# Batch 0's first product by halves of the depth, over eight PSUM banks, from a second layout of W

## The reference

```python
# x: (8, 256, 1024) f32; weight: (8, 1024, 1024); ids: 8 adapter numbers, one for each batch
y      = einsum('bsi,boi->bso', x, weight[ids])          # first product, W of the batch's adapter
base   = einsum('bth,oh->bto', y, W_up)                  # second product, the same W_up for all
logits = y @ gate_w.T + expert_bias                      # 4 experts
z      = einsum('nh,erh->ner', y, lora_A)                # rank 8 for each expert
delta  = einsum('ner,ehr->neh', z, lora_B)[argmax(logits)]
out    = x + base + delta
```

## Time and profile before

| what | us |
|---|---|
| median of 3 runs (367.38 to 367.71) | 367.55 |
| profiled execution, its own time | 367.27 |
| its span | 365.5 |
| PE busy | 360.0 (99%) |
| DVE, ACT busy | 279.6 (77%), 159.6 (44%) |

### The profile page before, as it was taken

The page is one execution under the profiler, slowest core; times in us unless marked ns, Lnnn a source line. Parts: engine busy times, 40 slices in busy tenths (PEclk is TensorE's granted clock), DMA queues, the critical chain, the costliest instruction groups (busy, mean ns, idle before and its releaser), DMA issues.

```text
span 365.5 us, 5961 instructions
## 1 busy us (share of the span) xinstructions
PE 360.0 (99%) x2180; PEld 322.5 (88%) x2180; DVE 279.6 (77%) x554; ACT 159.6 (44%) x318; POOL 1.3 (0%) x11
## 2 busy tenths in 40 slices
PE   7999999999999999999999999999999999999996
PEld 5888988899888998889988898889988899888995
DVE  4777889999987886579856788477984788755773
ACT  5677445963345521565024651255413652144300
POOL 0000000000000000000000000000000000000000
PEclk9999999999999999999999999999999999999999
DMA  7999987871049802676037750486305871160003
GB/s 242 392 401 292 404 355 289 307 264 65 1 174 343 269 21 104 207 275 223 0 130 249 256 174 2 172 295 201 138 2 203 313 231 61 57 231 1 2 0 115
DMA packets 20252, 68.16 MB, mean 187 GB/s; under 512 B 2304, under 2 KB 2688, under 8 KB 20224
## 3 DMA queue, kind: packets, MB, share of 16 engines
q1 hardware_dynamic: 19936, 66.74, 51.0%
q10 hardware_dynamic: 288, 1.05, 0.9%
HBM read 59.39 MB, written 8.39 MB: 185 GB/s over the span
## 4 chain that ended last, share of the span: by engine, by line
PE 97%; SPq 1%; DMA 1%; DVE 0%; ACT 0%; issue 0%
PE ps_y L806 33%; PE ps_y L809 16%; PE ps_u L817 13%; PE ps_v L817 7%; PE ps_p L817 6%; PE ps_u L823 3%; PE ps_u L825 3%; PE ps_u L827 3%; PE ps_v L823 2%; PE ps_v L827 2%; PE ps_v L825 2%; PE ps_p L823 1%; PE ps_p L825 1%; PE ps_p L827 1%; DMA w_raw<-w_dram 1%; SPq L240 1%
## 5 line engine op out<-in xcount | busy, mean ns | idle before, releaser
L806 PE MATMUL ps_y<-x_hilo,w_hi 128*128 128x512 f32 x512 | 160.9, 396 | 0.5 <-DVE w_lo L497 0.5
L809 PEld LDWEIGHTS ps_y<-x_hilo,w_lo 128*128 128x128 f32 x512 | 96.2, 188 | 22.7
L809 PE MATMUL ps_y<-x_hilo,w_lo 128*128 128x256 f32 x512 | 100.6, 278 | 0.0
L504 DVE TENSOR_TENSOR w_lo<-w_raw,w_hi 128x512 fp32r<-128x512 f32 x126 | 81.2, 689 | 11.5 <-ACT w_hi L372 10.8
L806 PEld LDWEIGHTS ps_y<-x_hilo,w_hi 128*128 128x128 f32 x512 | 78.4, 189 | 1.4 <-DVE w_lo L497 0.9
L372 ACT CAST w_hi<-w_raw 128x512 fp32r<-128x512 f32 x126 | 71.8, 624 | 3.2 <-DMA w_raw<-w_dram 3.2
L387 ACT COPY small<-ps_y 128x256 f32<-128x256 f32 x64 | 23.9, 373 | 98.3 <-PE ps_y L809 98.3
L556 DVE TENSOR_TENSOR y_raw<-ps_y,small 128x256 f32<-128x256 f32 x64 | 27.1, 424 | 43.3 <-ACT small L387 43.3
L817 PE MATMUL ps_u<-wide_hi,y_parts 128*128 128x256 f32 (+1 forms) x256 | 46.2, 288 | 0.0
L817 PEld LDWEIGHTS ps_u<-wide_hi,y_parts 128*128 128x128 f32 x256 | 38.5, 188 | 0.7
L390 ACT CAST y_parts<-y_raw 128x512 fp32r<-128x512 f32 x53 | 30.6, 619 | 12.1 <-DVE y_raw L562 12.1
(11 more groups left out here) (94 smaller groups left out, 380.7 us busy)
## 6 DMA issues: line engine op xcount, KB each, us to landing
w_raw<-w_dram SPq DMA_DIRECT2D x64, 512.0 KB, 4.8
rows<-x_dram SPq DMA_DIRECT2D x16, 512.0 KB, 6.2
out_dram<-rows SPq DMA_DIRECT2D x15, 512.0 KB, 2.7
x_raw<-xT_dram SPq DMA_DIRECT2D x14, 512.0 KB, 5.0
wide_raw<-w_up_dram SPq DMA_DIRECT2D x4, 512.0 KB, 12.1
thin_raw<-w_up_dram SPq DMA_DIRECT2D x4, 512.0 KB, 13.0
wide_stage<-w_up_dram SPq DMA_DIRECT2D x4, 512.0 KB, 12.8
thin_stage<-w_up_dram SPq DMA_DIRECT2D x4, 512.0 KB, 8.2
```

The lines of the kernel that those rows point to most:

```text
L504: dve.tensor_tensor(w_lo[:, n % RAWS, part], w_raw[:, n % RAWS, part], w_hi[:, n % RING, part].bitcast(F32), ALU.subtract).then_inc(w_read ...
L806: pe.matmul(ps_y[c % 2][:, :], w_hi[:, n % RING, i * P:(i + 1) * P], x_hilo[:, :, i, :], start=(i == 0), stop=False)
L809: last = pe.matmul(ps_y[c % 2][:, S:2 * S], w_lo[:, n % RAWS, i * P:(i + 1) * P], x_hilo[:, 0, i, :], start=False, stop=(i == KC - 1))
```

## The change

- W for batch 0 comes from a new input, `w_halves`. Row n of an adapter (0 to 7) still has 128 partitions of 4 KB, but holds half of the depth (four steps of k) of two neighbouring blocks: rows 0 to 3 are k = 0 to 3 of blocks 0-1, 2-3, 4-5, 6-7, and rows 4 to 7 are k = 4 to 7 of the same. Row 0 comes in two transfers of 256 KB, one for each of its blocks, in pieces of 2 KB. All later batches use `w` as before.
- `open_product()` takes the place of `first_product(0)` on PE: the half h of the depth is outside, the block c inside, each block with a PSUM bank of its own: the six of `ps_u`, `ps_v`, `ps_p` and the two `ps_y`. Block 0's hi matmuls wait for the hi part alone. `half_done` counts pairs of blocks done in the first half, `block_done` whole blocks in the second.
- The waits for a free slot of `w_raw` or `w_hi` go by `wait_for_use`, which counts `half_done` for rows 0 to 3 and `block_done` by two for rows 4 to 7.
- ACT and DVE split row 0 as 256, 256 and 512 columns, then rows 1 and 2, then x 3, then rows 3, 4, 5, unit 0, row 6, unit 1, ahead of the product's loop. Row 7 is split at c = 0, unit 2 at c = 2, the gate's parts at c = 3.
- `plain(0)` also waits for six blocks read out (`y_full_ready` 6), since they lie in its banks. `y_small(0, c)` waits for block c-2's addition.
- `gl` is issued ahead of unit 3. `WARM` is 11, not 18.

```diff
+        ps_open = [ps[:, i, :] for ps in (ps_u, ps_v, ps_p) for i in range(2)] + [ps[:, :] for ps in ps_y]
+        def wait_for_use(engine, n):
+            if n < OC // 2:
+                engine.wait_ge(half_done, n + 1)
+            elif n < OC:
+                engine.wait_ge(block_done, 2 * (n - OC // 2) + 2)
+            else:
+                engine.wait_ge(block_done, n + 1)
-            i = load_blocks(0, 4, i)
+            for n in range(4):
+                load_pair(n, i)
             for n in range(4, OC):
                 load_unit(n - 4)
-                i = load_blocks(n, n + 1, i)
-            sp.dma_start(gl_raw[:, 0:2 * Q, :], gl[:, :, :]).then_inc(gl_in, 16)
+                load_pair(n, i)
+                if n == 6:
+                    sp.dma_start(gl_raw[:, 0:2 * Q, :], gl[:, :, :]).then_inc(gl_in, 16)
-            for q in range(QUARTERS // 2):
-                first_w_hi(q)
+            first_w_hi()
+            for n in (1, 2):
+                w_hi_part(n)
             x_hi(0, XQ - 1)
-            for q in range(QUARTERS // 2, QUARTERS):
-                first_w_hi(q)
-            for n in range(1, AHEAD):
+            for n in (3, 4, 5):
                 w_hi_part(n)
+            unit_hi(0)
+            w_hi_part(6)
+            unit_hi(1)
+            def open_product():
+                for h in range(HALVES):
+                    for c in range(OC):
+                        m = h * OC + c
+                        n = m // 2
+                        for k in range(h * HK, (h + 1) * HK, 2):
+                            if c == 0:
+                                pe.wait_ge(x_ready, k // XK + 1)
+                            if m > 0:
+                                pe.wait_ge(w_ready, 2 * (m + 1))
+                            else:
+                                pe.wait_ge(w_hi_ready, k // QK + 1)
+                            at = [(c % 2 * HK + i % HK) * P for i in (k, k + 1)]
+                            for i in range(2):
+                                pe.matmul(ps_open[c], w_hi[:, n % RING, at[i]:at[i] + P], x_hilo[:, :, k + i, :],
+                                          start=(k + i == 0), stop=False)
+                            if m == 0:
+                                pe.wait_ge(w_ready, k // QK + 1)
+                            for i in range(2):
+                                last = pe.matmul(ps_open[c][:, S:2 * S], w_lo[:, n % RAWS, at[i]:at[i] + P],
+                                                 x_hilo[:, 0, k + i, :], start=False, stop=(k + i == KC - 1))
+                        if h == 1:
+                            last.then_inc(block_done, 1)
+                        elif c % 2 == 1:
+                            last.then_inc(half_done, 1)
                 if b == 0:
                     pe.wait_ge(gl_ready, 2)
+                    pe.wait_ge(y_full_ready, 6)
```

More of the change, by code:

```diff
@@ L23, with build @@
 B12 = T4
-def build(nc, xT, x, ids, w, w_up, gl, lora_b, bias, out):
+def build(nc, xT, x, ids, w, w_halves, w_up, gl, lora_b, bias, out):
     B, S, H = x.shape
@@ L62, in splits_at @@
     def splits_at(b, c):
+        if b == 0:
+            return (OC - 1,) if c == 0 else ()
         n = b * OC + c + AHEAD
@@ L160, in build @@
         rows_in = [sem(f"rows_in{t}") for t in range(T)]
+        w_half_in = sem("w_half_in")
+        half_done = sem("half_done")
         gl_in = sem("gl_in")
@@ L247, in load_w, with load_pair @@
                 if n >= RAWS:
-                    sp.wait_ge(block_done, n - RAWS + 1)
+                    wait_for_use(sp, n - RAWS)
                 sp.dma_start(w_raw[:, n % RAWS, :], w[bass.ds(i * OC + n % OC, 1), :, :].rearrange("a p n -> (a p) n")
                              ).then_inc(w_raw_in[n % RAWS], 16)
+            def load_pair(n, i):
+                if n >= RAWS:
+                    wait_for_use(sp, n - RAWS)
+                for a in range(2 if n == 0 else 1):
+                    part = slice(a * HK * P, (a + 1) * HK * P) if n == 0 else slice(0, KC * P)
+                    sp.dma_start(w_raw[:, n % RAWS, part],
+                                 w_halves[bass.ds(i * OC + n, 1), :, part].rearrange("a p n -> (a p) n")
+                                 ).then_inc(w_half_in if n == 0 and a == 0 else w_raw_in[n % RAWS], 16)
             def load_x(b):
@@ L386, in y_small @@
                 act.wait_ge(block_done, b * OC + c + 1)
-                act.copy(small[:, c % 2, :], ps_y[c % 2][:, S:2 * S]).then_inc(y_small_ready, 1)
+                if b == 0 and c >= 2:
+                    act.wait_ge(y_full_ready, c - 1)
+                act.copy(small[:, c % 2, :], y_bank(b, c)[:, S:2 * S]).then_inc(y_small_ready, 1)
             def y_hi_part(p):
@@ L492, in x_lo, with first_w_lo @@
                                   ALU.subtract).then_inc(x_ready, 1)
[L494 to L498, removed]
+            def first_w_lo():
+                for first, stop, count in ((0, QK, 1), (QK, HK, 2), (HK, KC, 4)):
+                    dve.wait_ge(w_hi_ready, count)
+                    part = slice(first * P, stop * P)
+                    dve.tensor_tensor(w_lo[:, 0, part], w_raw[:, 0, part], w_hi[:, 0, part].bitcast(F32), ALU.subtract
+                                      ).then_inc(w_ready, 2 if first == HK else 1)
             def w_lo_part(n):
@@ L767, in _ @@
                 x_lo(0, q)
-            for q in range(QUARTERS // 2):
-                first_w_lo(q)
+            first_w_lo()
+            for n in (1, 2):
+                w_lo_part(n)
             x_lo(0, XQ - 1)
-            for q in range(QUARTERS // 2, QUARTERS):
-                first_w_lo(q)
-            for n in range(1, AHEAD):
+            for n in (3, 4, 5):
                 w_lo_part(n)
+            unit_lo(0)
+            w_lo_part(6)
+            unit_lo(1)
             for b in range(B):
@@ L956, in _ @@
             for b in range(B):
-                first_product(b)
+                if b == 0:
+                    open_product()
+                else:
+                    first_product(b)
                 if b < PLAIN:
```

32 lines of the change are left out of this document (18 added, 14 removed).

## The result

| | median us | runs | profiled execution | its span |
|---|---|---|---|---|
| before | 367.50 (367.3 to 368.5) | 20 | 367.27 | 365.5 |
| changed | 368.09 (367.33 to 370.14) | 20 | 367.90 | 366.1 |

The changed kernel is slower: the ratio is 1.0018, 95% interval 1.001 to 1.0026, 0.6 us where a gain of 0.65 was forecast. Its times are also spread wider.

The account below looks back on a forecast made before the run. PE, busy 99% of the span, was taken as the bound, so only its stream's start counts: effective start 8.60 to 7.95, limited by P1, gains 0.65, taking 367.55 to 366.9; range 366.4 to 367.9.

Parts of the forecast that it names:

- P0a: First 256 KB transfer of W's row 0: landing taken as 6.9, effective start from it 7.55 (7.1 to 8.1).
- the first real matmul at 7.4: Opening on PE: block 0's hi matmuls start at 7.4, after P0a's cast ends at 7.34.
- P2: Transfer of W's row 2: taken to land at 11.65, effective start 7.61, 0.34 in hand.
- half block 2: Third 1.39 us piece of PE's stream, fed by P1: start 10.73, effective start (10.73 less 2.78) 7.95.
- the term for P1: Transfer of W's row 1: lands at 9.2 as W 1 did, ends last and sets effective start 7.95.
- rival 2: DMA-rate gap falls wholly into P1, or P2 slips over 0.34: gain 0 to 0.4, 367.4; chance 0.17.
- Rival 3: Cut of row 0 costs a fixed part: P0b at 9.1, P1 at 10.6, 0.75 slower, 368.3; chance 0.04.
- P0b: Second 256 KB transfer of row 0: landing taken as 7.7, effective start 7.84 (7.64 to 8.04).
- The rival: Rival 5, clock in the opening: idle PE falls back to 1.2 GHz, losing 1.5, 368.4; chance 0.04.
- the cover of 0.5: Handover to the second product: the sixth addition ends at 29.8, 0.5 before PE asks at 30.35; no stall.
- P7 landed 23.2: Last row of batch 0's W: landing at 23.2, needed at 27.4; input to the handover's chain on ACT.
- The 0.65: Whole gain forecast: effective start of PE's stream moves from 8.60 to 7.95, all kept to the end.

Follow-up runs that it names:

- row 0 whole: Changed kernel with W's row 0 in one 512 KB transfer, not two: 367.30 beside 367.30 with 18 warm-ups, 367.73 beside 367.50 with 11.
- two transfers by partition: Row 0 whole, 18 warm-ups, row 7 early, but row 0 in two transfers of 64 partitions, 4 KB pieces: 368.87 beside 367.45.
- row 7 early: Changed kernel with row 7 of W issued ahead of gl and unit 3: 368.11 beside 367.52; with row 0 whole and 18 warm-ups 367.25, again 367.06.
- x late: Changed kernel with x's second half loaded behind P1: 369.23 (row 0 whole, 18 warm-ups), 369.82 (cut, 18), 368.63 (whole, 14), beside 367.37.

## Why the prediction was wrong

**Right.** PE is the path to the end, and nothing but the start of the stream and its breaks counts: in every profile the second product's start moves as the time does. P0a was taken at 6.9 and its cast began at 7.03 and 7.15 in the two profiles; the first real matmul at 7.4 came at 7.58 and 7.70. P2, P3 and the later rows had time. P7's load had its place in the queue as forecast, though it was issued at 12.52 and 12.55 and not at 11.9; in the first profile it waited 0.7 behind the slow PE, where I had no wait. That P1 ends last was right too, and the arithmetic from landing to half block 2 holds: 1.53 forecast, 1.48 in the second profile (10.40 to 11.88) and 1.47 with 18 warm-ups (10.78 to 12.25).

**The step that failed** is the term for P1: "The bytes ahead of P1 are the same, and its issue moves from 4.8 to 5.35, well ahead of its data ... I take 9.2." The bytes were the same and the landing wasn't. P1 reached ACT at 10.15 and 10.40 in the two profiles of the changed kernel, and the second block of W at 10.76 to 11.35 in the five others with row 0 or W 0 cut along the depth and W first in the queue. With it whole it was 9.24 to 9.97 in five profiles of the changed order, and at 9.43 at the latest in the kernel before, whose cast waited for ACT; the one exception is the kernel before with 11 warm-ups, whole and at 11.28. P1 in the changed kernel is 0.95 and 1.20 later than the 9.2; at one to one that is the 0.65 lost, and 0.3 and 0.55 more. I read W 0 and W 1 landing 1.7 apart as "transfers in flight share their fixed part"; the row held for those two, and I carried it to three. I had the price nearly right under rival 2 (effective 8.5 from 9.8), named the dip as its mechanism, and gave it 0.17 with 0 to 0.4 of gain as the worst, since I priced it as the part of a fixed gap that W 1 hadn't already paid, and not as a dip that the cut moves ahead of P1.

The rule of the Trainium skill that I set aside ("DMA: Bandwidth & Descriptors", section Bandwidth: batch DMAs to at least 1 MiB) pointed the right way, and the runs agree: 0.46 to 0.89 slower with the cut. Rival 3, its mechanism, had 0.04; its time, 368.3, was nearest to the 368.09 measured, but its form varied: in the two profiles of the changed kernel P0b was there within 0.76 of P0a, so the two halves overlapped and the cost fell on P1; in the other kernels with this cut the cast of P0b began 1.1 to 2.3 behind P0a's.

**The clock.** The removed warm-ups were booked at nothing, "in PE's idle head". In the first profile the clock was released only at 11.3, and this cost 0.5 on top of P1; in the kernel with row 0 whole it fell back to the 1.2 GHz level. The rival had 0.04 and a price of 1.5. The price is what the kernel before with 11 warm-ups paid, in five of twelve executions; with row 0 whole it was 0.7 in three of eleven. In the median it is worth 0.2 to 0.4 with row 0 whole, within the measurement's interval. In the changed kernel the mean of 0.995 is seen once in 30 executions, the slowest (370.14), though an execution whose clock is released late reads 1.00 and can't be counted so; with 18 warm-ups in their place its median doesn't move. P1's landing can cover most of what a slow opening costs, all but 0.5 in the first profile, but no run shows that this is the reason. Two readings failed here. I took the release from one profile as fixed, and it isn't: over the profiles the 18 warm-ups took from 5.74 to 7.10 us, and in three of five profiles with 11 all of them were slow. And I took PE's idle stretch of 0.46 before 8.45 as evidence for a longer one; released clocks did pass stretches of 1.4 (two transfers by partition) and 1.6 (row 7 early) without a fall, and one of 2.1 not.

**The handover.** The chain of ACT was right from its start to its end, and the cover of 0.5 as well. What failed was its input, "P7 landed 23.2": issued at 12.5 in both profiles of the changed kernel, it came at 23.6 and 25.7. The price was 0.7 in one of the two; with x late it was 1.6 behind a row 7 at 27.0. In the changed kernel's median it is at most 0.1; in the cut kernel with 18 warm-ups 0.3 to 0.5.

**The halves of the depth themselves** do what the forecast said, about half as much: with row 0 whole, 18 warm-ups and row 7 early, the kernel gains 0.27 and 0.39 against the one before, by a second product from 30.78 and 30.71 in place of 31.01. Without row 7 early they gain nothing that can be measured. The 0.65 assumed a first matmul at 7.4 and P1 at 9.2; in the faster of the two the first matmul is at 8.15, 0.4 behind the warm-up's end, since row 0 whole reaches ACT at 7.6, and P1 at 9.5.

## What to carry to other kernels

Where a kernel starts on its first loads, the transfer behind them matters as much as the first: a cut that brings the first half 0.5 us earlier can put the next transfer 1 us later, and a schedule that consumes it sooner has lost the time that used to hide this. When matmuls are removed from a warm-up, look at the distance between matmuls in the opening, not at PE's busy share or the list of waits: both looked clean while the opening ran at half rate. And a landing time read from one profile is one draw: a chain that rests on it with 0.5 us of cover wants the transfer moved ahead of whatever isn't needed first.

## What the runs showed of the hardware

- The same 512 KB, issued at 4.3, were usable at 7.6 in one transfer, at 7.75 in one transfer of 2 KB pieces, and at 9.85 in two transfers of 64 partitions each.
- The DMA rate falls twice in the opening. Between 5.0 and 6.0 it is low with the cut and without (205 and 205 GB/s in the changed kernel, 254 and 262 in the kernel before). Between 6.5 and 10.0 it falls again, in most profiles for 1 to 1.5 us, to 49 to 172 GB/s in the lowest half microsecond, from about 400 ahead of it.
- The clock column reads 1.00 in openings where matmuls of 512 columns start 0.43 apart (the 1.2 GHz level); in the one profiled execution whose clock was released and fell again, it reads 0.50 from 8.3 to 11.7. The distance between matmuls is the safer reading.
- The clock's release isn't at a fixed time: 18 warm-ups from 1.96 on took 5.74 us in one profile and 7.10 in another, with more of them at the 1.2 GHz level in the second.
- Row 7, issued at 12.52 and at 12.55 in two executions of one kernel, reached ACT at 23.6 and 25.7. What decides between the two stays open.
